# First layer of the feed-forward part on pairs of tiles with 256 moving columns, with new places in the order of the work and the closing recurrence mixed on VectorE

## What is computed

```python
x = layernorm(x + attention(x))          # 16 heads of 16, one key and one value head shared by all
x = layernorm(x + ffn(x))                # gelu(x @ T(W1).T + b1) @ T(W2).T + b2, T makes weights -1, 0 or 1; 1024 hidden
x = layernorm(x + ssm_and_cfc(x))        # inner layernorm, states by a cumulative sum over positions, then
                                         # a recurrence h = ff1*(1-t) + t*ff2 over all 512 positions, then out_w
x = layernorm(x + quantised_linear(x))   # blocks of 32 rounded to a 6-bit grid, 256 x 256 weights
```

## Time and profile before

| | |
|---|---|
| median of 3 runs | 1774.13 us (1772.9 to 1775.65) |
| the profiled execution | 1771.39 us |
| its span, first to last instruction | 1769.6 us |
| mean granted TensorE clock | 0.966 of full |
| busy PE / PEld / DVE / ACT / POOL | 1637.5 / 1189.0 / 1343.4 / 1293.2 / 1104.3 us |
| first exponential of tile 0, 10, 63 | 97.4, 337.7, 1637.7 us |

### The profile page before, as it was taken

The page is one execution under the profiler, slowest core; times in us unless marked ns, Lnnn a source line. Parts: engine busy times, 40 slices in busy tenths (PEclk is TensorE's granted clock), DMA queues, the critical chain, the costliest instruction groups (busy, mean ns, idle before and its releaser), DMA issues.

```text
span 1769.6 us, 84556 instructions
## 1 busy us (share of the span) xinstructions
PE 1637.5 (93%) x35371; PEld 1189.0 (67%) x35371; DVE 1343.4 (76%) x2605; ACT 1293.2 (73%) x2601; POOL 1104.3 (62%) x3392
## 2 busy tenths in 40 slices
PE   5768999999999999999999999999999999999865
PEld 4535667677777777677777777777777767776643
DVE  5546778888788888888888888888888888887454
ACT  3437777788787888778887778887788877887521
POOL 5002346767677776676777767777677776767732
PEclk8879999999999999999999999999999999999875
DMA  9963334444244433444333444334443344431010
GB/s 239 203 93 54 60 58 62 74 72 69 51 72 73 73 66 58 67 73 72 70 61 62 74 72 69 61 62 74 71 71 61 62 71 71 73 58 32 18 29 20
DMA packets 133765, 125.18 MB, mean 71 GB/s; under 512 B 18965, under 2 KB 130633, under 8 KB 133385
## 3 DMA queue, kind: packets, MB, share of 16 engines
q1 hardware_dynamic: 129184, 119.50, 39.1%
q10 hardware_dynamic: 4200, 0.27, 0.2%
HBM read 33.73 MB, written 18.87 MB: 30 GB/s over the span
## 4 chain that ended last, share of the span: by engine, by line
PE 53%; POOL 15%; ACT 10%; issue 8%; DVE 4%; DMA 4%; SPq 4%; POOLq 0%; DVEq 0%; ACTq 0%
PE value_bank L772 11%; PE gen_bank L910 8%; PE score_banks L750 7%; PE gen_bank L598 6%; PE max_banks L590 6%; PE gate_bank L803 5%; ACT L1130 4%; ACT probs L1130 3%; PE gen_bank L819 3%; PE gate_bank L598 2%; POOL square L1613 2%; POOL rstd L1598 2%; DMA key_pieces<-khalf 2%; POOL diff L1717 2%; POOL hseq L1722 2%
## 5 line engine op out<-in xcount | busy, mean ns | idle before, releaser
L1186 DVE TENSOR_REDUCE nmax<-max_banks 128x2 f32<-128x1024 f32 x512 | 622.5, 1216 | 65.3 <-PE max_banks L592 61.3
L1130 ACT ACTIVATE probs<-score_banks 128x1024 f32<-128x1024 f32 x512 | 525.0, 1025 | 112.3 <-PE score_banks L752 96.3
L772 PE MATMUL value_bank<-probs,vaug 128*32 128x128 f32 x8192 | 327.3, 278 | 1.1 <-issue 1.1
L772 PEld LDWEIGHTS value_bank<-probs,vaug 128*32 128x32 f32 x8192 | 205.5, 110 | 90.6 <-issue 79.7
L590 PE MATMUL max_banks<-kaug,qaug 62*128 62x512 f32 x512 | 238.7, 466 | 24.8 <-DVE nmax L1186 15.7
L750 PE MATMUL score_banks<-qaug,kaug 64*128 64x512 f32 x512 | 237.6, 464 | 12.4 <-ACT probs L1130 7.8
L1717 POOL TENSOR_TENSOR diff<-gates 128x16 f32<-128x16 f32 x472 | 114.2, 242 | 212.3 <-ACT gates L1135 205.1
L592 PE MATMUL max_banks<-kaug,qaug 62*128 62x512 f32 x512 | 239.2, 467 | 0.4 <-issue 0.4
L752 PE MATMUL score_banks<-qaug,kaug 64*128 64x512 f32 x512 | 237.6, 464 | 0.0
L1135 ACT ACTIVATE gates<-gate_bank 128x48 f32<-128x48 f32 x472 | 99.0, 210 | 167.6 <-PE gate_bank L803 167.2
L803 PEld LDWEIGHTS gate_bank<-hseq,ghT 128*32 128x32 f32 x11328 | 159.1, 112 | 81.3 <-POOL hseq L1722 57.4
(11 more groups left out here) (234 smaller groups left out, 3540.6 us busy)
## 6 DMA issues: line engine op xcount, KB each, us to landing
qstage<-qhalf SPq DMA_DIRECT2D x384, 128.0 KB
qstage<-qhalf SPq DMA_DIRECT2D x128, 112.0 KB
xt<-in_L_attn_x SPq DMA_DIRECT2D x64, 128.0 KB
xk<-in_L_attn_x SPq DMA_DIRECT2D x16, 512.0 KB, 8.7
residual<-x2s SPq DMA_DIRECT2D x64, 128.0 KB
x2f<-residual SPq DMA_DIRECT2D x64, 128.0 KB
out<-x SPq DMA_DIRECT2D x64, 128.0 KB
qaug<-nmT SPq DMA_DIRECT2D x256, 8.0 KB, 1.8
```

The costliest lines, as they stand in the source:

```text
L772: last = pe.matmul(value_bank[32 * g:32 * g + 32, :].rearrange("p (k t) -> p k t", k=HG)[:, :, u * BLOCK_POS:(u + 1) * BLOCK_POS], vaug[:, ...
L1130: act.activation(probs[:, beat % 2, :, :], score_banks[:, :, :], ACT.Exp).then_inc(exp_done, 1)
L1186: dve.tensor_reduce(nmax[:, m % 2, at:at + 9:8], max_banks[:, :, :], AX_X, ALU.max, negate=True).then_inc(max_taken, 1)
```

## The change

- **First layer on pairs.** x1 is split in two fp32r halves (`x1half`) and kept for two tiles. The weights are kept as fp32r (`w1T` for `w1Tb`). At tile time of j, half of the hidden blocks is made for both tiles of a pair: 16 matmuls of 256 moving columns per tile in place of 48 of 128. The gelu is four operations of 256 columns. The second layer adds half of the hidden blocks for both tiles, in the two halves of the bank, 16 matmuls per tile as before; its sum is taken in one operation of 512 columns (`X2R`), once into `x1b` and once into `x2r`, and the statistics (`ST2`) stand apart from it.
- **Leads.** `PAIRED=-2`, `SUM=-3`, `SSM=-4`, `REC=-8`, `OUT=-9`: state part, recurrence and last layer run two tiles later.
- **Places.** All tables have new numbers. `OWN_AT` has numbers of their own for tile times 0 to 7 (and for the two before them), in which parts are still missing. What follows tile 63 is now one stage of 4 x 256 slots (`CLOSING_AT`), in place of tile time 64 and the piece `TAIL_SSM` of the tail.
- **Closing.** The closing stage has the 32 steps of tiles 56 to 59, mixed on DVE in three operations; the tail keeps 32 steps (tiles 60 to 63) in place of 40.
- **Quarters.** Only the pieces in `QUARTERED` are made in quarters; the last layer (`LAST`) is now made with whole weights.

```diff
-LEAD = dict(LOAD=4, X=3, Q=2, MAX=1, ATTN=0, FFN=-1, SSM=-2, REC=-6, OUT=-7)
+LEAD = dict(LOAD=4, X=3, Q=2, MAX=1, ATTN=0, FFN=-1, PAIRED=-2, SUM=-3, SSM=-4, REC=-8, OUT=-9)
...
-    MIX=(3, 4, 12, 13, 20, 34, 96, 157),
+    MIX=(9, 37, 71, 90, 91, 100, 116, 128),
 )
+OWN_AT = {
...
+    1: dict(
+        PE=dict(XT=75, Q=0, OT=81, ATT=87, PROJ=150, X1T=214, NM=178),
...
+CLOSING_AT = dict(
...
+    SP=dict(X2F=(109, 250, 253, 273), STORE=(101, 245, 253, 391), OUTST=(99, 251, 253, 270)),
...
+QUARTERED = ("INPUT", "Q", "OUT", "PROJ", "B")
-TAIL_SSM = dict(F2=0, X2R=0, LN2=0, X2=2, X2S=2, XN=4, TURN=4, COPY=4, B=5, BS=5, SCAN=6)
...
-        w1Tb = sb("w1Tb", [P, KT, F], BF16)
+        w1T = sb("w1T", [P, KT, F], F32R)
...
+            def multiplied(name, out, weights, moving, start, stop):
+
+                if name not in QUARTERED:
+                    return pe.matmul(out(slice(0, P)), weights, moving, start=start, stop=stop, skip_group_check=True)
...
-            def second_layer(f):
-                pe.matmul(gen_bank[0][:, 0:D], hhi[:, f, :], w2T[:, f, :], start=(f == 0), stop=False, skip_group_check=True)
-                return pe.matmul(gen_bank[0][:, 0:D], hlo[:, f, :], w2T[:, f, :], start=False, stop=(f == FT - 1), skip_group_check=True)
+            def second_layer(j, i):
+
+                f, t = divmod(i, 2)
+                out = gen_bank[0][:, t * D:(t + 1) * D]
+                of_f = w2T[:, FT // 2 * (j % 2) + f, :]
+                pe.matmul(out, hhi[:, i, :], of_f, start=(i == 0), stop=False, skip_group_check=True)
+                return pe.matmul(out, hlo[:, i, :], of_f, start=False, stop=(f == FT // 2 - 1), skip_group_check=True)
+
+            def first_layer(j, bank):
+
+                p, half = divmod(j, 2)
+                for at in range(2):
+                    f = FT // 2 * half + 2 * bank + at
+                    for piece in range(2):
+                        for k in range(KT):
+                            last = pe.matmul(gen_bank[bank][:, at * 2 * P:(at + 1) * 2 * P], w1T[:, k, f * P:(f + 1) * P],
+                                             x1half[:, p % 2, piece, k, :, :].rearrange("p t s -> p (t s)"),
+                                             start=(piece + k == 0), stop=(piece + k == 2), skip_group_check=True)
+                return last
...
-                            for f in range(4):
-                                ft = 4 * half + f
-                                last = act.activation(hT[:, ft, :], gen_bank[half][:, f * P:(f + 1) * P], ACT.Gelu, bias=cols[:, C_B1 + ft:C_B1 + ft + 1])
+                            for i in range(2):
+                                f = FT // 2 * (m % 2) + 2 * half + i
+                                in_h = slice(4 * half + 2 * i, 4 * half + 2 * i + 2)
+                                last = act.activation(hT[:, in_h, :].rearrange("p t s -> p (t s)"), gen_bank[half][:, i * 2 * P:(i + 1) * 2 * P],
+                                                      ACT.Gelu, bias=cols[:, C_B1 + f:C_B1 + f + 1])
...
-                        dve.tensor_tensor(x1rest[:, :, :], g0[:, 0:D].rearrange("p (k t) -> p k t", k=KT), x1piece[:, 0, :, :],
-                                          ALU.subtract).then_inc(emptied[0], 1)
...
-                        dve.tensor_copy(x1piece[:, 1, :, :], x1rest[:, :, :]).then_inc(x1_step, 1)
...
-                        dve.tensor_tensor(x1piece[:, 2, :, :], x1rest[:, :, :], x1piece[:, 1, :, :], ALU.subtract).then_inc(x1_step, 1)
...
+                        dve.tensor_tensor(x1half[:, m // 2 % 2, 1, :, m % 2, :], g0[:, 0:D].rearrange("p (k t) -> p k t", k=KT),
+                                          x1half[:, m // 2 % 2, 0, :, m % 2, :], ALU.subtract).then_inc(emptied[0], 1)
...
+                    beat = beat_at("MIX", n, at) if n == TILES else None
+                    if beat is not None:
+                        j = STEPS * REC_CLOSING + beat
+                        mix(j, j // STEPS % HELD, j % STEPS)
```

438 lines of the change are left out of this document (252 added, 186 removed).

## The result

| | before | changed |
|---|---|---|
| median | 1774.66 us (4 runs, 1772.9 to 1775.65) | 1733.18 us (4 runs, 1729.94 to 1739.06) |
| ratio, 95% interval | | 0.9771 [0.9743, 0.9799] |
| profiled execution, its span | 1771.39, 1769.6 us | 1734.31, 1732.6 us |

Faster by 2.3%, 41 us. The forecast was 1685 us with a range of 1654 to 1722: the sign was right, the size was not, and the result lies outside the range. So what one occasion says of this kernel is uncertain by some 0.3% more than its interval shows, and I judge small differences by stages of the traces, one trace for each kernel.

The account below looks back on a forecast made before the run. The prediction took PE to bound the full stage; 1769.6 - 62 (full stage) - 35 (first ten tiles) + 8 (behind tile 63) gave a span of 1680.6 us, hence a median of 1685 us, range 1654 to 1722.

Parts of the forecast that it names:

- What bounds the kernel: In the 53 full-stage tile times PE, busy 24.07 of 24.53 us per tile, was taken as the bound.
- First layer, PE: First-layer block on PE: 16 matmuls at 0.117 us, 1.88 us, replace 3.05 us, saving 1.17 us per tile.
- Rival 3: Every first layer: weight loads do not hide, 1.85 us more per block, about 1874 us in all; chance 0.04.
- Other engines: Per tile DVE ends some 0.8 us lower and ACT 0.7 us; worth nothing in themselves, they keep covers.
- Full stage: 53 tile times fall from 24.53 to 23.36 us each, -62 us, with bounds of -31 and -74.
- Rival 1: Full stage: saved PE time turns into waits, half the saving is lost, 1716 us in all; chance 0.15.
- Idle time: PE's idle time in the full stage stays at 0.46 us per tile.
- First ten tiles: The first ten tile times fall from 240.3 to 205.5 us, -35 us, with bounds of -22 and -45.
- Behind tile 63: After tile 63's start: 32 steps and the last pair's chain take about 50 us, +8 us; bounds 0 and +30.
- one rival at a time: 1716: full-stage saving half lost, chance 0.15; 1710: first tiles do not shrink, chance 0.12; 1722: the range's upper end.

Follow-up runs that it names:

- before_less: The kernel before with 32 of the 48 bfloat16 matmuls of its first layer; 1780.46 us, ratio 1.0024.
- no_load: The changed kernel with the first layer's gelus computed as tanh, so that two table loads of 1.28 us per tile go; 1713.01 us, ratio 0.9639.
- old_places: The changed kernel with the full-tile places of the kernel before; pairs, leads, first tiles and closing as changed; 1754.90 us, ratio 0.9821.
- half_first: The changed kernel with 8 of the 16 first-layer matmuls, without the low half of x1; 1743.99 us, ratio 0.9814.
- no_own: The changed kernel with the first tiles' own table emptied, so that they take the full tile's places; 1748.31 us, ratio 0.9858.

## Why the prediction was right and wrong, step by step

**What bounds the kernel: wrong.** "So there PE is the bound, and time taken from PE comes off if nothing else is late" is the step that failed. The 24.07 of 24.53 us that PE is busy were read as a bound; before_less shows 0.45 us less of it worth nothing, and no_load shows that busy time itself shrinks by 20 us with no matmul less. The page had it: nearly half of the chain lay off PE, most of that on POOL and ACT.

**First layer, PE: mechanism right, size a little off.** 2.15 us where I had 1.98; the loads hide, at 0.117 us apart. Rival 3 is out.

**Other engines: "worth nothing in themselves" is where the gain was misplaced.** With less on PE alone nothing comes; with less on ACT and DVE too, 22 us come in the one trace of old_places.

**Full stage: -46, not -62.** In place of my 1.17 us per tile stand 0.87, by old_places' trace 0.42 from the pairs and 0.45 from new places, for which I had allowed only half of the idle time as a bound. Rival 1, with 0.15, was nearer to the mechanism: saved PE time turns into waits on ScalarE (half_first). Its 31 us were too many for this stage; the new places gave back part of what the rings took, which is luck for a forecast that had not priced them.

**Idle time: right for no good reason.** 0.42 us per tile, forecast 0.46. PE's idle time does not tell whether it bounds.

**First ten tiles: -16, not -35.** Tile times 0 to 9 took 25.6, 21.1, 19.5, 20.3, 20.7, 21.2, 21.8, 21.5, 25.6 and 27.2 us, forecast 24, 17, 17.7, 19.2, three of 20.3, 20.8, 22.5 and 23.4. I had taken off each part's PE time; in no_own, where that time is gone but the own orders are missing, 2 us are left of it, and the rest of what there is comes from the orders. Two terms hold most of the miss: tile time 1 (4.1 us), where eight maxima of 1.83 us were a floor and not a length, and tile times 8 and 9 (6.9 us), where places made for the full tile meet one that is not full.

**Behind tile 63: +24, not +8.** 60.7 us from oT to the last states where I had 50. I had taken the longer of two lengths, 49 for the steps and 47.7 for the chain of the last pair. With the mixing off the ring there are still 55.8. If that is the chain of the last pair, it was priced some 8 us too short, and steps and chain add up in part, in one fixed order on engines that both use; I had that as a bound (+30) and not as the case. No run takes the steps out altogether, so how the 11 us divide stays open. Then the 32nd step ends after the states, not with them: 17.2 us from the last states to the end of tile 60 where before it was 12.8 (3.4 of it for what is left of tile 59, and 13.8 for tile 60, at a granted clock of 0.50). The tail's 36.60 and 19.90 us came as forecast. What I said of the mixing (DVE 49, POOL 54) had the right sign and a third of the size: 15 us.

**The range.** It let one rival at a time come true (1716, 1710, 1722). Three terms missed by 16 to 19 us each, all the same way, and together they are the 48 us.

## What to carry to other kernels

An engine busy for 98% of a stage is a bound only where the chain of waits stays on it: add the chain up by engine over some periods before an edit is priced by its engine's time, and ask what the second and third ring would give. In this kernel, whose order is fixed, several rings lie within 1 to 2% of each other, so that work taken from one engine gave nothing, work added to it cost nearly in full, and the gain came with less work on several at once and a new order. A busy share does not tell this apart, since it stretches with the stage. Places that fit the steady state need not fit the periods before it.
